# First loads divided over two DMA queues with the input in front, and the first transposes taken token tile by token tile

## Chip, core and metric

One core of one Trainium2 chip runs the whole kernel. The metric is the device time of one execution in microseconds, the median of several runs. The engines are TensorE (PE, with its weight loads shown apart as PEld), VectorE (DVE), ScalarE (ACT), GpSimd (POOL) and SyncE (SP), which here only issues DMAs.

## What is computed

The input `x` is 8 batches of 100 tokens of 512 features, the context 8 x 722 x 512. A decoder layer (self-attention, cross-attention, feed-forward, each with a residual sum and a layer norm) and then a mixture of experts are added to `x`:

```python
x = x + _L0_xattn_ref(_layernorm(x), ctx_1024, ...)
x = x + _L0_ffn_ref(_layernorm(x), Wg, w1, w2)
```

The part that the change touches is the very first: `_layernorm(x)`, and beside it the product of two weight matrices, value projection by output projection (`in_proj_w[2D:]` and `out_proj_w`), which the kernel makes once and uses in place of both.

## The kernel before

All large matrix products run in TensorE's fp32r form in three passes: each fp32 operand is split into a high part (ScalarE copies it, rounding to fp32r) and a low part (VectorE or GpSimd subtracts the high part from the original), and PE multiplies high by high, high by low and low by high. The 800 tokens stand in two halves of 400 (4 batches of 100 tokens). The instructions of each engine are written out in one fixed order, and semaphores tie the engines together; there is no planner. All loads are issued by SyncE on its one queue, in the order of the code.

The head of the program, until PE comes to the first product with the input (`unit(U_Q, 0)`, line 1105), goes as follows.

- **SP** loads quarter 0 and 1 of the two combined weights (`VR` and `OR`, four 256 KB chunks each, `load_vo(0)`, `load_vo(1)`), then the first half of `x` (`load_x_tail(0)`, 32 KB, and `load_x(0)`, `load_x(1)`, 384 KB each, 96 partitions), then `load_vo(2)`, `load_vo(3)`, then the first weights of the query unit (`WR`), the second half of `x`, the constants, and the key weights (`WRK`, 1 MB, line 527).
- **ACT** makes `VH` and `OH` of the four chunks in turn (`split_vo(k)`, lines 1406 and 1408), then half of the first normalisation (token tiles 2 and 3, line 1320), `WH` of the query weights, `XH` of the transposed input (line 1329), more `WH`, then the high part of the combined weights (line 1420), then `WH` of the key weights.
- **DVE** follows with the low parts `VL` and `OL` and, written behind `split_v(1)`, the statistics of the first four token tiles (line 1721), then its half of the normalisation (token tiles 0 and 1, line 1743), then `XL` (line 1759), then two chunks of the query weights' `WL` (line 1917).
- **POOL** makes `OL` of chunks 1 and 3 (`split_o`), the power `rstd` between them (line 636, `inverse_deviation`), and two chunks of the query weights' `WL` (line 642).
- **PE** runs 11 warm-up products on the identity (line 1098), then for each of the four chunks 4 products high by high (`combine_high`, line 929), 4 low by high (line 935) and 4 high by low (line 941). Between the high products and the low products of chunk 3 stand the 16 transposes of the first half of `x` (`to_features(0, 0)`, line 884). They run feature chunk by feature chunk, each over the four token tiles, and every feature chunk is announced as it is done (`to_feat`); `norm_features` on ACT and DVE takes them up one by one.

The second half of the tokens is normalised in the same manner during `unit(U_Q, 0)` and the first group of `unit(U_K, 0)`, and `to_features(0, 1)` (line 1107) transposes it. Its `rstd` on POOL stands behind the key weights' `WL` chunks 2 and 3 (line 707), and these behind ACT's split of the key weights.

Of the kernel before, what the change touches and what calls it, by code (L numbers as in the profile page):

```python
# [7 lines left out]
ALU = mybir.AluOpType  # L8
# [4 lines left out]
P = 128  # L13
B, T, D = 8, 100, 512
# [5 lines left out]
HB = B // 2  # L20
KC = D // P
# [6 lines left out]
TA = T // 16 * 16  # L28
# [144 lines left out]
def build(nc, x, ctxt, ctxn, wvo, wts, consts, g3, be3, out):  # L173
    with ExitStack() as ctx:
        def sem(name):
            return ctx.enter_context(nc.semaphore(name))
# [10 lines left out]
        def sb(name, region, offset, shape, dt=F32):  # L187
            return nc.alloc_sbuf_tensor_at(name, shape, dt, offset=at[region] + offset)
# [19 lines left out]
        tok = sb("tok", "R3", 0, [T, B, D])  # L208
# [37 lines left out]
        VR, OR = [sb(name, "R2", o, [P, KC, D]) for name, o in (("VR", 0), ("OR", 8192))]  # L246
        off = [0]

        def small(name, shape, dt=F32):
            size = 4  # L250
            for s in shape[1:]:
                size *= s
            t = sb(name, "C", off[0], shape, dt)
            off[0] += (size + 31) // 32 * 32
            return t

        ident = small("ident", [P, P])
# [14 lines left out]
        rstd = small("rstd", [T, B])  # L272
# [12 lines left out]
        ps = ctx.enter_context(nc.psum_tensor("ps", [P, 8, 512], F32))  # L285


        x_loaded = [sem("x_loaded%d" % i) for i in range(4)]
        x_tail = [sem("x_tail0"), sem("x_tail1")]
        v_loaded = [sem("v_loaded%d" % k) for k in range(KC)]  # L290
        o_loaded = [sem("o_loaded%d" % k) for k in range(KC)]
# [34 lines left out]
        stats_ready = sem("stats_ready")  # L326
        nmr_ready = sem("nmr_ready")
        tok_ready = sem("tok_ready")
        to_tok = sem("to_tok")
        to_feat = sem("to_feat")  # L330
        x_affine = sem("x_affine")
# [167 lines left out]
        def _(sp):  # L499
            def load_x(i):  # L500
                sp.dma_start(tok[0:TA, 2 * i:2 * i + 2, :], x[2 * i:2 * i + 2, 0:TA].rearrange("b t d -> t b d")
                             ).then_inc(x_loaded[i], 16)

            def load_x_tail(h):

                bs = slice(HB * h, HB * (h + 1))
                sp.dma_start(tok[TA:T, bs, :], x[bs, TA:T].rearrange("b t d -> t b d")).then_inc(x_tail[h], 16)

            def load_vo(k):

                sp.dma_start(VR[:, k, :], wvo[0, :, k, :]).then_inc(v_loaded[k], 16)
                sp.dma_start(OR[:, k, :], wvo[1, :, k, :]).then_inc(o_loaded[k], 16)

            load_vo(0)
            load_vo(1)
            load_x_tail(0)
            load_x(0)
            load_x(1)
            load_vo(2)
            load_vo(3)  # L520
            sp.dma_start(WR[:, 0:2, :], wts[0, :, 0:2, :]).then_inc(w0_loaded, 16)
# [103 lines left out]
        def _(pool):  # L625
# [8 lines left out]
            def inverse_deviation(i, h):  # L634
                pool.wait_ge(stats_ready, i + 1)
                pool.tensor_tensor(rstd[:, HB * h:HB * (h + 1)], veps[:, :], nhalf[:, :],  # L636
                                   ALU.pow).then_inc(rstd_ready, 1)
# [12 lines left out]
            def split_o(k):  # L650

                pool.wait_ge(o_high, k + 1)
                pool.tensor_tensor(OL[:, k, :], OR[:, k, :], raw(OH[:, k, :]), ALU.subtract).then_inc(o_low_pool, 1)
# [45 lines left out]

            split_o(1)  # L700
            inverse_deviation(0, 0)
            pool.wait_ge(nmr_ready, 1)
            split_o(3)
            split_weights(U_Q, range(KC // 2))
            for k in range(KC // 2, KC):
# [48 lines left out]
        def _(pe):  # L754
# [120 lines left out]

            def to_features(i, h, tiles):

                pe.wait_ge(tok_ready, 8 * i + HB * (h + 1))
                if i == 0 and h == 1:
                    pe.wait_ge(vo_low, KC)  # L880
                first = 0 if i == 0 and h == 0 else 4
                for k in range(KC):
                    for j in range(HB):
                        mm = pe.transpose(ps[:, first + k, j * T:(j + 1) * T], tiles[:, j, k * P:(k + 1) * P],  # L884
                                          ident[0:T, 0:T])
                    mm.then_inc(to_feat, 1)

            def to_tokens(i, h, n, src, chunks=range(KC)):

                for k in chunks:  # L890
                    pe.wait_ge(dve_evac, dve_count(n, h, k))
                    if (i, h, k) == (4, 1, KC - 1):
                        pe.wait_ge(out_ready, 2 * HB)
                    for j in range(HB):
                        if (i, h, k, j) == (4, 1, KC - 1, HB // 2):
                            pe.wait_ge(dve_evac, dve_count(n, h, k) + 1)

                        if k:
                            pass
                        elif i == 2 and h == 0:  # L900
                            pe.wait_ge(*((c_exp, B) if j < 2 else (c_probT_low, B)))
                        elif i == 4 and h == 1:
                            pe.wait_ge(out_ready, j + 1)
                        elif h == 1:
                            pe.wait_ge(x_ready, 8 * i + j + 1)
                            if i == 3:
                                pe.wait_ge(x_copied, j + 1)
                        else:
                            pe.wait_ge(x_ready, 8 * min(i, 4))
                        mm = pe.transpose(ps[0:T, 4 + j, k * P:(k + 1) * P], src[h][:, k, j * T:(j + 1) * T],  # L910
                                          ident[:, :])
                        if k == KC - 1 or (i, h, k) == (4, 1, KC - 2):
                            mm.then_inc(to_tok, 1)
# [11 lines left out]
            def combine_high(k):  # L925

                pe.wait_ge(o_high, k + 1)
                for e in range(KC):
                    pe.matmul(ps[:, 4 + e, :], VH[:, k, e * P:(e + 1) * P], OH[:, k, :], start=(k == 0), stop=False)

            def combine_low(k):

                pe.wait_ge(v_low, k + 1)
                for e in range(KC):
                    pe.matmul(ps[:, 4 + e, :], VL[:, k, e * P:(e + 1) * P], OH[:, k, :], start=False, stop=False)
                if k % 2 == 0:
                    pe.wait_ge(o_low, k // 2 + 1)
                else:
                    pe.wait_ge(o_low_pool, k // 2 + 1)
                for e in range(KC):  # L940
                    mm = pe.matmul(ps[:, 4 + e, :], VH[:, k, e * P:(e + 1) * P], OL[:, k, :], start=False,
                                   stop=(k == KC - 1))
                    if k == KC - 1:
                        mm.then_inc(vo_made, 1)
# [146 lines left out]
            tiles = [tok[:, 0:HB, :], tok[:, HB:B, :]]  # L1091
# [7 lines left out]
            for k in range(KC - 1):  # L1099
                combine_high(k)  # L1100
                combine_low(k)
            combine_high(KC - 1)
            to_features(0, 0, tiles[0])
            combine_low(KC - 1)
            unit(U_Q, 0)
            unit(U_K, 0, [0])
# [90 lines left out]
        def _(act):  # L1197
# [116 lines left out]
            def normalise(i, h, dst):  # L1314

                act.wait_ge(nmr_ready, 2 * i + h + 1)
                for j in range(HB // 2, HB):
                    b = HB * h + j
                    src = tok[:, b, :] if i in (0, 3) else ps[0:T, 4 + j, :]
                    act.activation(dst[:, j, :], src, ACT.Identity, bias=nmr[:, b:b + 1],  # L1320
                                   scale=rstd[:, b:b + 1]).then_inc(tok_ready, 1)

            def norm_features(i, h):
                for k in range(KC):
# [76 lines left out]
            tiles = [tok[:, 0:HB, :], tok[:, HB:B, :]]  # L1401
            tiles2 = [tok2[:, 0:HB, :], tok2[:, HB:B, :]]

            def split_vo(k):
                act.wait_ge(v_loaded[k], 16)
                act.activation(VH[:, k, :], VR[:, k, :], ACT.Copy).then_inc(v_high, 1)
                act.wait_ge(o_loaded[k], 16)
                act.activation(OH[:, k, :], OR[:, k, :], ACT.Copy).then_inc(o_high, 1)

            for k in range(KC):  # L1410
                split_vo(k)
            normalise(0, 0, tiles[0])
# [132 lines left out]
        def _(dve):  # L1545
# [188 lines left out]
            def normalise(i, h, dst):  # L1734

                dve.wait_ge(rstd_ready, {0: h, 1: 2 + h, 2: 4 + h, 3: 7 + 2 * h}[i] + 1)
                cols = slice(HB * h, HB * (h + 1))
                dve.scalar_tensor_tensor(out=nmr[:, cols], in0=mv[:, cols, 0], scalar=-1.0, in1=rstd[:, cols],
                                         op0=ALU.mult, op1=ALU.mult).then_inc(nmr_ready, 1)
                for j in range(HB // 2):  # L1740
                    b = HB * h + j
                    src = tok[:, b, :] if i in (0, 3) else ps[0:T, 4 + j, :]
                    dve.tensor_scalar(dst[:, j, :], src, mv[:, b, 0:1], rstd[:, b:b + 1], ALU.subtract,
                                      ALU.mult).then_inc(tok_ready, 1)

            def affine_features(i, h, chunks=(1, 3)):

# [147 lines left out]
            tiles = [tok[:, 0:HB, :], tok[:, HB:B, :]]  # L1895
# [219 lines left out]
```

## Time and profile before

| what | value |
|---|---|
| runs before | 516.28, 516.35, 516.75 us; median 516.35 us |
| the profiled execution | 516.95 us, of which its span (first to last instruction) is 515.1 us |
| PE busy in the span | 505.2 us (98%) |
| DVE, ACT, POOL busy | 374.1, 242.4, 141.4 us (73%, 47%, 27%) |
| DMA | 53.76 MB, 104 GB/s over the span |

The span is what the trace shows; 1.85 us of the profiled execution lie around it. PE's busy share says that nearly all of the time is set by PE; the small rest is idle time of PE, and the rows below show the part of it that lies at the head.

### The profile page before, as it was taken

Reading aid. Unit: us, or ns where it says so; the run is one execution under the profiler, and the core shown is the slowest. Engines: PE = TensorE matmul, PEld = TensorE weight load, DVE = VectorE, ACT = ScalarE, POOL = GpSimd, SP = SyncE. Lnnn points to the kernel's source line nnn. Section 1 sums busy time; section 2 is a strip of 40 time slices with the busy share of each in tenths; the row PEclk is TensorE's granted clock in tenths of the full one; section 3 lists DMA queues with packets and bytes.
Section 4 is the critical chain, followed back from the end, with each engine's and each line's share of the span. In section 5 each row is a group of like instructions: output and inputs, shape, how many; then the busy total and the mean of one; then the engine's idle time right before and its main releaser. Section 6 shows DMA issues by size and latency. Waiting matters only on the chain.

```text
span 515.1 us, 7631 instructions
## 1 busy us (share of the span) xinstructions
PE 505.2 (98%) x2958; PEld 484.4 (94%) x2958; DVE 374.1 (73%) x643; ACT 242.4 (47%) x429; POOL 141.4 (27%) x105
## 2 busy tenths in 40 slices
PE   7999999999999999999999999999999999999997
PEld 6899999889988888989999999999999899999996
DVE  3853769796798986786499877368586878786645
ACT  3853652465598976164554333205437532442210
POOL 2430540014023135154504000805337404030000
PEclk9999999999999999999999999999999999999999
DMA  8951122031689871214522242001301021202004
GB/s 222 337 211 59 59 83 81 1 115 59 223 290 329 298 231 38 81 48 114 92 83 81 83 163 67 16 2 53 111 1 48 36 83 62 102 0 83 1 1 129
DMA packets 18444, 53.76 MB, mean 104 GB/s; under 512 B 1640, under 2 KB 2440, under 8 KB 15848
## 3 DMA queue, kind: packets, MB, share of 16 engines
q1 hardware_dynamic: 18348, 53.20, 31.1%
q8 instruction: 24, 0.39, 0.3%
q14 instruction: 12, 0.10, 0.1%
q10 hardware_dynamic: 60, 0.07, 0.1%
HBM read 51.63 MB, written 1.64 MB: 103 GB/s over the span
## 4 chain that ended last, share of the span: by engine, by line
PE 89%; DVE 4%; DMA 3%; ACT 2%; issue 1%; SPq 0%; POOL 0%; DVEq 0%; ACTq 0%
PE ps L798 17%; PE ps L800 17%; PE ps L799 17%; PE ps L856 5%; PE ps L855 5%; PE ps L854 5%; PE ps L910 2%; PE ps L884 2%; PE ps L1052 2%; PE ps L1053 2%; PE ps L1054 2%; DMA tok<-x_in 2%; PE ps L1026 2%; PE ps L1028 2%; PE ps L1027 2%; PE ps L998 1%
## 5 line engine op out<-in xcount | busy, mean ns | idle before, releaser
L798 PE MATMUL ps<-AH,WH 128*128 128x400 f32 x284 | 98.9, 348 | 1.3 <-DVE AL L1583 1.1
L800 PE MATMUL ps<-AH,WL 128*128 128x400 f32 x284 | 98.0, 345 | 0.0
L799 PE MATMUL ps<-AL,WH 128*128 128x400 f32 x284 | 97.9, 345 | 0.0
L798 PE MATMUL ps<-XH,WH 128*128 128x400 f32 x192 | 66.8, 348 | 0.1
L800 PE MATMUL ps<-XH,WL 128*128 128x400 f32 x192 | 66.3, 345 | 0.0
L799 PE MATMUL ps<-XL,WH 128*128 128x400 f32 x192 | 66.2, 345 | 0.0
L642 POOL TENSOR_TENSOR WL<-WR,WH 128x512 fp32r<-128x512 f32 x30 | 43.3, 1470 | 68.5 <-ACT WH L1217 68.5
L798 PEld LDWEIGHTS ps<-AH,WH 128*128 128x128 f32 x284 | 53.3, 188 | 2.8 <-DVE AL L1583 2.6
L799 PEld LDWEIGHTS ps<-AL,WH 128*128 128x128 f32 x284 | 53.4, 188 | 0.0
L800 PEld LDWEIGHTS ps<-AH,WL 128*128 128x128 f32 x284 | 53.4, 188 | 0.0
L1217 ACT ACTIVATE WH<-WR 128x512 fp32r<-128x512 f32 x60 | 34.1, 624 | 24.3 <-DMA WR<-wts_in 24.3
L1296 ACT ACTIVATE AH<-AT 128x400 fp32r<-128x400 f32 x40 | 21.2, 538 | 49.3 <-DVE AT L1643 32.4
L1605 DVE TENSOR_TENSOR acc<-ps,acc 128x400 f32<-128x400 f32 x47 | 26.7, 570 | 18.7 <-PE ps L800 18.5
L1562 DVE TENSOR_TENSOR ctL<-ctR,ctH 128x1444 fp32r<-128x1444 f32 x16 | 27.9, 1750 | 13.3 <-ACT ctH L1225 13.3
L798 PEld LDWEIGHTS ps<-XH,WH 128*128 128x128 f32 x192 | 36.1, 188 | 0.7 <-issue 0.3
L799 PEld LDWEIGHTS ps<-XL,WH 128*128 128x128 f32 x192 | 36.1, 188 | 0.0
L800 PEld LDWEIGHTS ps<-XH,WL 128*128 128x128 f32 x192 | 36.1, 188 | 0.0
L647 POOL TENSOR_TENSOR cnL<-cnR,cnH 128x1024 fp32r<-128x1024 f32 x7 | 17.0, 2435 | 53.8 <-ACT cnH L1231 53.8
L636 POOL TENSOR_TENSOR rstd<-veps,nhalf 100x4 f32<-100x4 f32 x10 | 14.0, 1395 | 59.3 <-DVE veps L1731 59.0
L1247 ACT ACTIVATE AT<-ps,cst 128x400 f32<-128x400 f32 x16 | 9.5, 595 | 43.7 <-PE ps L800 43.6
L1648 DVE SCALAR_TENSOR_TENSOR AL<-AT,AH 128x400 fp32r<-128x400 f32 x40 | 27.8, 715 | 1.6
L1231 ACT ACTIVATE cnH<-cnR 128x1024 fp32r<-128x1024 f32 x24 | 24.7, 1058 | 1.1 <-DMA cnR<-ctxn_in 1.1
(244 smaller groups left out, 1189.3 us busy)
## 6 DMA issues: line engine op xcount, KB each, us to landing
WR<-wts_in SPq DMA_DIRECT2D x19, 1024.0 KB, 4.8
ctR<-ctxt_in SPq DMA_DIRECT2D x16, 722.0 KB, 5.9
cnR<-ctxn_in SPq DMA_DIRECT2D x16, 512.0 KB, 5.1
cnR<-ctxn_in SPq DMA_DIRECT2D x8, 256.0 KB
tok<-x_in SPq DMA_DIRECT2D x4, 384.0 KB, 10.1
tok<-x_in SPq DMA_DIRECT2D x1, 1536.0 KB
cnR<-ctxn_in SPq DMA_DIRECT2D x8, 160.0 KB
VR<-wvo_in SPq DMA_DIRECT2D x4, 256.0 KB, 6.9
```

Of the source, the lines that this page charges most:

```text
L642: pool.tensor_tensor(WL[SLOT[n]][:, k, :], WR[:, k, :], raw(WH[SLOT[n]][:, k, :]), ALU.subtract).then_inc(w_low_pool, 1)
L798: pe.matmul(dst, wh, half(mh, h, k), start=(k == 0), stop=False)
L799: pe.matmul(dst, wh, half(ml, h, k), start=False, stop=False)
L800: mm = pe.matmul(dst, wl, half(mh, h, k), start=False, stop=(k == KC - 1))
L854: pe.matmul(dst, ah[:, k, cols], bh[:, k, :], start=(k == 0), stop=False)
L855: pe.matmul(dst, ah[:, k, cols], bl[:, k, :], start=False, stop=False)
L856: mm = pe.matmul(dst, al[:, k, cols], bh[:, k, :], start=False, stop=(k == 1))
L1217: act.activation(WH[SLOT[n]][:, k, :], raw_weights[:, k, :], ACT.Copy).then_inc(w_high, 1)
L1231: act.activation(cnH[:, 2 * i:2 * i + 2, :], raw_cn(b, i), ACT.Copy).then_inc(cn_high, 1)
L1562: dve.tensor_tensor(ctL[b % 2][:, 2 * i:2 * i + 2, 0:M], raw_ct(b, i), raw(ctH[b % 2][:, 2 * i:2 * i + 2, 0:M]), ALU.subtract).then_inc(ct ...
L1605: dve.tensor_tensor(half(acc, h, e), src, half(acc, h, e), ALU.add).then_inc(dve_evac, 1)
L1648: dve.scalar_tensor_tensor(out=half(AL, h, e), in0=half(AT, h, e), scalar=0.0, in1=raw(half(AH, h, e)), op0=ALU.max, op1=ALU.subtract).the ...
```

## The change

The first half of `x` is loaded in front of everything else: its first 384 KB and the 32 KB tail by SP, its second 384 KB by ACT's queue, before ACT's first activation. Chunks 0 and 1 of `OR` follow on ACT's queue; the other loads keep their order on SP's. PE's first 16 transposes go token tile by token tile, each tile behind a wait for its own normalisation (new semaphores `first_dve` and `first_act` count tiles 0, 1 and tiles 2, 3), and all four feature chunks are announced during the last tile. POOL's `split_o(3)` waits until DVE has normalised both its tiles, where it waited for the small product `nmr` ahead of them. The orders of ACT's, DVE's and PE's instructions are otherwise the same. The wait in `to_features` drops by four because the first half no longer counts in `tok_ready`.

```diff
+        first_dve, first_act = sem("first_dve"), sem("first_act")
...
-            load_vo(0)
-            load_vo(1)
+            load_x(0)
             load_x_tail(0)
-            load_x(0)
-            load_x(1)
+            load_v(0)
+            load_v(1)
             load_vo(2)
             load_vo(3)
...
             split_o(1)
             inverse_deviation(0, 0)
-            pool.wait_ge(nmr_ready, 1)
+            pool.wait_ge(first_dve, HB // 2)
             split_o(3)
...
             def to_features(i, h, tiles):
-                pe.wait_ge(tok_ready, 8 * i + HB * (h + 1))
+                pe.wait_ge(tok_ready, 8 * i + HB * h)
...
+            def first_features(tiles):
+
+                for j in range(HB):
+                    if j < HB // 2:
+                        pe.wait_ge(first_dve, j + 1)
+                    else:
+                        pe.wait_ge(first_act, j - HB // 2 + 1)
+                    for k in range(KC):
+                        mm = pe.transpose(ps[:, k, j * T:(j + 1) * T], tiles[:, j, k * P:(k + 1) * P],
+                                          ident[0:T, 0:T])
+                        if j == HB - 1:
+                            mm.then_inc(to_feat, 1)
...
             combine_high(KC - 1)
-            to_features(0, 0, tiles[0])
+            first_features(tiles[0])
             combine_low(KC - 1)
...
+            act.dma_start(tok[0:TA, 2:4, :], x[2:4, 0:TA].rearrange("b t d -> t b d")).then_inc(x_loaded[1], 16)
+            for k in range(2):
+                act.dma_start(OR[:, k, :], wvo[1, :, k, :]).then_inc(o_loaded[k], 16)
             for k in range(KC):
                 split_vo(k)
             normalise(0, 0, tiles[0])
```

## Rows read from the trace of the kernel before

**Rows 1.** The page: busy time of each engine.
```profile
PE 505.2 (98%) x2958; PEld 484.4 (94%) x2958; DVE 374.1 (73%) x643; ACT 242.4 (47%) x429; POOL 141.4 (27%) x105
```

**Rows 2.** Timeline of PE, 0 to 21.5 us: start, us, what, idle before.
```profile
1.73 4.27 PE L1098 MATMUL ps<-ident 128*128 128x128 f32 x22 [1.73 <-POOL ones L632]
5.75 1.17 PE L929 MATMUL ps<-OH,VH 128*128 128x512 f32 x4
...
9.20 1.20 PE L929 MATMUL ps<-OH,VH 128*128 128x512 f32 x4 [0.46 <-ACT OH L1408]
10.23 1.07 PE L935 MATMUL ps<-OH,VL 128*128 128x512 f32 x4
11.14 1.07 PE L941 MATMUL ps<-OL,VH 128*128 128x512 f32 x4
...
17.98 1.59 PE L884 MATMUL ps<-ident,tok 100*128 100x100 f32 x16 [0.38 <-DVE tok L1743]
...
19.36 1.17 PE L935 MATMUL ps<-OH,VL 128*128 128x512 f32 x4
...
21.29 0.34 PE L798 MATMUL ps<-XH,WH 128*128 128x400 f32 x1
```

**Rows 3.** The chain that ended last, in order of time: start, us, what.
```profile
3.37 8.47 DMA tok<-x_in
...
32.41 1.38 PE ps L884 x16
```

**Rows 4.** Timeline of ACT, 0 to 32 us.
```profile
4.80 0.63 ACT L1408 ACTIVATE OH<-OR 128x512 fp32r<-128x512 f32 x1 [0.21 <-DMA OR<-wvo_in]
7.15 0.63 ACT L1406 ACTIVATE VH<-VR 128x512 fp32r<-128x512 f32 x1 [1.72 <-DMA VR<-wvo_in]
8.51 0.63 ACT L1408 ACTIVATE OH<-OR 128x512 fp32r<-128x512 f32 x1 [0.73 <-DMA OR<-wvo_in]
12.32 0.63 ACT L1406 ACTIVATE VH<-VR 128x512 fp32r<-128x512 f32 x1 [3.18 <-DMA VR<-wvo_in]
...
18.58 1.69 ACT L1329 ACTIVATE XH<-ps 128x400 fp32r<-128x400 f32 x4
...
23.88 2.20 ACT L1217 ACTIVATE WH<-WRK 128x512 fp32r<-128x512 f32 x4 [0.51 <-DMA WRK<-wts_in]
...
30.53 1.52 ACT L1320 ACTIVATE tok<-tok,nmr,rstd 100x512 f32<-100x512 f32 x2 [1.87 <-DVE nmr L1738]
```

**Rows 5.** Timeline of DVE, 0 to 22 us.
```profile
10.48 2.67 DVE L1721 BATCH_NORM_STATS2 bnst<-tok 100x6 f32<-100x512 f32 x4 [1.97 <-DMA tok<-x_in]
...
15.95 1.98 DVE L1743 TENSOR_SCALAR tok<-tok,mv,rstd 100x512 f32<-100x512 f32 x2
...
21.05 1.28 DVE L1917 TENSOR_TENSOR WL<-WR,WH 128x512 fp32r<-128x512 f32 x2
```

**Rows 6.** Windows: width, busy and (count) of PE, PEld, DVE, ACT, POOL, clock, DMA share, GB/s.
```profile
1.73:5.75 4.02, 4.02 (x22) 4.02 (x23) 0.98 (x2) 1.55 (x3) 0.41 (x1) 1.00 0.81 206
5.75:8.75 3.00, 2.98 (x15) 2.16 (x13) 1.09 (x2) 0.87 (x2) 0.00 (x0) 1.00 0.98 263
...
12.21:13.68 1.47, 0.00 (x0) 0.00 (x0) 1.40 (x8) 1.26 (x3) 0.00 (x0) 1.00 1.07 405
```

**Rows 7.** Windows, later stretch, while line 601 reloads all of x alone.
```profile
245.00:247.00 2.00, 2.00 (x13) 2.00 (x12) 0.00 (x0) 0.47 (x1) 1.92 (x2) 1.00 1.06 236
```

**Rows 8.** The warm-up's line: weight loads, ns min/median/max.
```profile
L1098 PEld LDWEIGHTS ps<-ident x22: 192/333/338, 1.7 to 5.6; 128*128 128x128 f32 x22
```

**Rows 9.** Tile tok: DVE's half of the normalisation, ns min/median/max.
```profile
L1743 DVE TENSOR_SCALAR tok<-tok,mv,rstd x4: 540/542/1519, 16.0 to 30.9; 100x512 f32<-100x512 f32 x4
```

**Rows 10.** Timeline of POOL, 0 to 21 us.
```profile
16.12 1.53 POOL L653 TENSOR_TENSOR OL<-OR,OH 128x512 fp32r<-128x512 f32 x1 [0.28 <-DVE nmr L1738]
18.19 2.74 POOL L642 TENSOR_TENSOR WL<-WR,WH 128x512 fp32r<-128x512 f32 x2 [0.55 <-ACT WH L1217]
```

**Rows 11.** Timeline of SP: its first DMA issue.
```profile
0.74 0.38 SPq L511 DMA_DIRECT2D VR<-wvo_in  x1
```

More of the change, by code:

```diff
@@ L507, in load_x_tail, with load_v @@
                 sp.dma_start(tok[TA:T, bs, :], x[bs, TA:T].rearrange("b t d -> t b d")).then_inc(x_tail[h], 16)
+            def load_v(k):
+                sp.dma_start(VR[:, k, :], wvo[0, :, k, :]).then_inc(v_loaded[k], 16)
             def load_vo(k):
-                sp.dma_start(VR[:, k, :], wvo[0, :, k, :]).then_inc(v_loaded[k], 16)
+                load_v(k)
                 sp.dma_start(OR[:, k, :], wvo[1, :, k, :]).then_inc(o_loaded[k], 16)
-            load_vo(0)
-            load_vo(1)
+            load_x(0)
             load_x_tail(0)
-            load_x(0)
-            load_x(1)
+            load_v(0)
+            load_v(1)
             load_vo(2)
@@ L876, in to_features @@
             def to_features(i, h, tiles):
-                pe.wait_ge(tok_ready, 8 * i + HB * (h + 1))
+                pe.wait_ge(tok_ready, 8 * i + HB * h)
                 if i == 0 and h == 1:
                     pe.wait_ge(vo_low, KC)
-                first = 0 if i == 0 and h == 0 else 4
                 for k in range(KC):
                     for j in range(HB):
-                        mm = pe.transpose(ps[:, first + k, j * T:(j + 1) * T], tiles[:, j, k * P:(k + 1) * P],
+                        mm = pe.transpose(ps[:, 4 + k, j * T:(j + 1) * T], tiles[:, j, k * P:(k + 1) * P],
                                           ident[0:T, 0:T])
                     mm.then_inc(to_feat, 1)
+            def first_features(tiles):
[9 more added lines that the diff above has]
+                            mm.then_inc(to_feat, 1)
             def to_tokens(i, h, n, src, chunks=range(KC)):
@@ L1320, in normalise @@
                     act.activation(dst[:, j, :], src, ACT.Identity, bias=nmr[:, b:b + 1],
-                                   scale=rstd[:, b:b + 1]).then_inc(tok_ready, 1)
+                                   scale=rstd[:, b:b + 1]).then_inc(first_act if (i, h) == (0, 0) else tok_ready, 1)
             def norm_features(i, h):
@@ L1743, in normalise @@
                     dve.tensor_scalar(dst[:, j, :], src, mv[:, b, 0:1], rstd[:, b:b + 1], ALU.subtract,
-                                      ALU.mult).then_inc(tok_ready, 1)
+                                      ALU.mult).then_inc(first_dve if (i, h) == (0, 0) else tok_ready, 1)
             def affine_features(i, h, chunks=(1, 3)):
```

## The prediction

> **What bounds the kernel now.** I read the page first: PE is busy for 505.2 of 515.1 us [rows 1], so a change is worth what it adds to or takes from PE's idle time, or what it does to the one stretch where PE waits for loads. That stretch is the head. PE's timeline there [rows 2] shows the warm-ups to about 5.75 us, the weight product from 5.75, waits of 0.46 us for `OH` of chunk 1 and of 1.47 us for chunk 2 [rows 2, 6], and 0.38 us ahead of the transposes, which begin at T = 17.98. These 2.3 us are all that better loading could give. `unit(U_Q, 0)` begins at 21.29 and the next hard dependency is the second block of transposes at 32.41 [rows 3].
>
> ACT's timeline [rows 4] then tells when loads land, as ACT takes each chunk up at once: `OR` 0 by 4.80 us, `VR` 1 by 7.15, `OR` 1 by 8.51, `VR` 2 by 12.32. The chain [rows 3] ends the second quarter of x at 3.37 + 8.47 = 11.84. In all of this the DMA engines are 0.8 to 1.07 busy [rows 6]: the head is bound by bytes in a queue, and their order decides.
>
> **The loads.** The weight product's first step needs `OH` 0, so `VR` 0 and `OR` 0. Before, 512 KB had to land for it. After, 384 + 384 + 32 KB of x are ahead of, and 512 KB with, these two: 1312 KB or 1.34 MB. Three readings of when that has landed:
> - Lowest. `OR` 0 landed at 4.8 after 0.52 MB; at the 405 GB/s of an x-free stretch [rows 6] that is 1.3 us of data, so the queue's dead time ends at 3.5. The two quarters of x took 11.84 - 8.51 = 3.34 us [rows 3, 4]; 0.79 MB in that time is 235 GB/s, and the reload of x alone, much later, runs at the same 236 [rows 7]. So x is a slow load in itself, and ends at 6.8. `VR` 2 stood 0.5 us behind the end of x before, and one more chunk costs 0.65: `OR` 0 at 8.0.
> - Bytes moved. 4.02 us x 206 = 0.83 MB by 5.75, then 263 GB/s [rows 6]: 1.34 MB moved at 7.7. Landing lags behind that: 1.05 MB (through `OR` 1) would be moved at 6.6 and landed at 8.5, 1.9 us later, since some engines run ahead. This gives 9.6.
> - Highest. Landing against bytes as it was: 1024 KB at 8.51, 1824 KB at 11.84, so 1312 KB at 9.7, with the tail at most 9.9.
>
> I take 8.8, between the first and the other two, as the start of x no longer mixes with chunks 1. Then ACT makes `VH` and `OH`: 0.67 us behind the landing if `VR` 0 is a little ahead, 1.3 us if both land together, which two queues with the same bytes ahead make likely. So the product starts at S = 9.9 where it was 5.75; bounds 8.7 and 11.2.
>
> **From there.** With no wait a chunk costs 2.85 us (9.20 to 12.05: a first group of 1.03, then 0.91 each [rows 2]), the next ones 3 x 0.91 = 2.73, the high group of chunk 3 0.91: 2.85 + 2.73 + 2.73 + 0.91 = 9.2. Chunk 1 is needed at S + 2.85 = 12.8, when ACT has long split it (four activations of 0.67 from 8.8 end at 11.5), and the rest of the queue runs at 405 GB/s; so the three waits, 2.3 us, do go. T becomes 9.9 + 9.2 = 19.1: +1.1 us. Bounds by S: 17.9 (-0.1) and 20.4 (+2.4).
>
> **x in front buys little by itself.** DVE's order is unchanged: the statistics stand behind `split_v(1)`, and that waits for ACT's third activation, `VH` 1, at about 10.6. `VL` 1 ends at about 11.3, so statistics start at about 11.3 where they started at 10.48 [rows 5]. From there to the normalisation it took 5.47 us (15.95 - 10.48 [rows 5]): 16.8, and the four tiles are ready at about 18.3. PE comes at 19.1 and doesn't wait. 0.8 us of cover; without it, with S at 8.7, all moves together and the cover is the same, since both hang on the same loads.
>
> **POOL's wait.** DVE's two tiles took 1.98 us [rows 5], one of them 1519 ns where the other three of this line took 540 [rows 9], while POOL's `OL` 3 ran from 16.12 to 17.65 [rows 10]. With POOL held back DVE needs 1.1 us: 0.9 us less on the way to the transposes, hidden here as PE is late. `OL` 3 ends 1.5 us behind DVE, at about 19.4; PE needs it at T + 1.4 + 0.9 = 21.4. Behind it on POOL stand the two `WL` of the query weights, 2.74 us [rows 10]: to 22.2, the first to about 20.8; PE wants them at 22.8 and 23.3. Covered. The Trainium skill, in "SBUF — State Buffer", section "Who interferes with whom", says that VectorE in its two-port modes and GpSimd lock each other out for a whole instruction; the 1519 ns agree, and the sum is the same without the rule.
>
> **ACT's issues.** Three DMA issues of about 0.4 us [rows 11] stand ahead of ACT's first activation, which has nothing to read before 4 us. Free.
>
> **Tile by tile.** The 16 transposes cost the same 1.38 us (17.98 to 19.36 [rows 2]). No tile is late, so the finer waits win nothing. But feature chunk 0 is announced after 13 of 16 instead of after 4 of 16: 9 x 0.086 = 0.78 us later relative to T. `XH` then starts at T + 1.38 (was 18.58 = T + 0.60 [rows 4]) and everything behind it on ACT and DVE moves too. `WL` 2 on DVE (21.05 [rows 5], T + 3.07) now starts at T + 3.85 and ends at T + 4.53; PE's third product of that chunk stands at T + 3.31 + 8 x 0.18 = T + 4.77. 0.24 us of cover, and 0.18 for `WL` 3. Further on, ACT reached the key weights at 23.37 and waited 0.51 us for them [rows 4]; now it is there at T + 5.39 + 0.78 = T + 6.17. From that start to the last normalised tile of the second half it took 30.53 + 1.52 - 23.88 = 8.17 us, so T + 14.34; PE wants it at T + 14.43 (32.41 [rows 3]). I put 0.1 us there, bounds 0 and 0.6 (if the 0.78 is paid in full again).
>
> **Sum.** +1.1 + 0.1 = +1.2 us on the profiled execution's 516.95 (span 515.1 and 1.85 around it), 518.15; the median stands 0.6 lower, so 516.35 + 1.2 = 517.6 us. Behind 33 us nothing differs and PE runs full, so the shift stays to the end. Own range of this case: S from 9.2 (T 18.4, +0.4) to 11.2 (+2.4), with the stall of 0 to 0.6: 516.8 to 519.3.
>
> **Rivals.**
> - *The clock falls.* PE is idle from 5.9 to about 9.9, 4 us; before, its longest pause was 1.47 us and its speed held. At the start, weight loads took 333 ns and from about 5 us on 192 [rows 8], the levels 1.2 and 2.4 GHz, though the clock column reads 1.00; it took some 3.2 us of work (1.73 to 5) to rise. The same again on the weight product, at half pace: +1.5 us, in all +2.7, 519.1. For: the pause is far longer than any seen. Against: no row shows a fall. The Trainium skill, "TensorE: Matmul & The Clock Gate", Part 1, has PE go back to 1.2 GHz after idling; no row of this trace shows it.
> - *The new order costs nothing.* The loads come near the low bound, S 8.7 to 9.2, and the waits removed pay for the late start: +0 to +0.5, 516.6.
> - *Faster.* Two queues move x faster than one. If x went at 405 GB/s as the chunks do, it would save 1.4 us of 3.34, and S is below 7.7; T is then 1.1 us or more earlier. It decides from S = 7.8. But the key weights at 23.86 bind next: without them also earlier, only 32.41 - 32.05 = 0.36 us is kept. With them, -1.2: 515.1. For: the two queues overlap the dead time of x. Against: the DMA engines show full shares with one queue already [rows 6, 7]. The Trainium skill, "DMA: Bandwidth & Descriptors", "Issuing engines are not separate DMA queues", says that several issuers save only issue time; nothing here shows two at once.
>
> **Chances.** What a measurement can tell is about 0.2%, 1.0 us. Forecast case 0.46 (of it 0.13 below +1.0), clock 0.17, nothing 0.25, faster 0.12. So faster 0.12, same 0.38, slower 0.50. Range 516.0 to 519.4, which leaves out most of the faster case and the worst of the clock.
>
> **What the changed profile would show.** First `OH` ending near 9.9 and PE idle from 5.9 to there, no idle time between chunks, transposes at about 19.1 with no wait on tiles, DVE's two tiles at 0.54 us each, `XH` 1.4 us behind the first transpose, the second transposes at about 33.6. The prediction is wrong if `OR` 0 lands before 7.5 or after 10, if weight loads of chunk 0 take 333 ns, or if statistics start later than 12 us, so that PE waits for tiles after all.

## The result and the profile after

The changed kernel takes 519.25 us (median of 6 runs, 518.67 to 519.66), the kernel before 516.65 us (median of 6 runs, 516.28 to 517.12). The ratio is 1.0048 with a 95% interval of 1.0037 to 1.0058: slower by 2.6 us. The forecast was 517.6 us, with a range of 516.0 to 519.4 and a chance of 0.50 for slower. The sign and the range hold; the shift is more than twice the 1.2 us of the forecast.

The page of the kernel after, busy time of each engine, answers to [rows 1]:

```profile
PE 506.8 (98%) x2958; PEld 486.2 (94%) x2958; DVE 372.9 (72%) x643; ACT 242.0 (47%) x429; POOL 141.3 (27%) x105
```

PE is busy for 1.6 us longer than before, with the same 2958 products, so some of them took longer. The timeline of PE (start, us, what, idle before) answers to [rows 2]:

```profile
1.73 4.88 PE L1114 MATMUL ps<-ident 128*128 128x128 f32 x22 [1.73 <-POOL ones L636]
10.16 2.08 PE L945 MATMUL ps<-OH,VH 128*128 128x512 f32 x4 [3.55 <-ACT OH L1424]
12.03 1.59 PE L951 MATMUL ps<-OH,VL 128*128 128x512 f32 x4
13.46 1.09 PE L957 MATMUL ps<-OL,VH 128*128 128x512 f32 x4
14.39 1.07 PE L945 MATMUL ps<-OH,VH 128*128 128x512 f32 x4
...
20.75 1.54 PE L899 MATMUL ps<-ident,tok 100*128 100x100 f32 x16
22.06 1.18 PE L951 MATMUL ps<-OH,VL 128*128 128x512 f32 x4
...
24.00 0.34 PE L802 MATMUL ps<-XH,WH 128*128 128x400 f32 x1
```

The warm-ups alone took 0.61 us longer (4.88 against 4.27 us); with 11 products they took 4.1 to 5.1 us in the profiles of this case, and the first chunk's start hangs on the loads here, not on them. The first chunk starts at 10.16 where it started at 5.75, after a pause of 3.55 us. Its groups of four take 2.08 and 1.59 us instead of 1.17 and 1.07, so that chunk 1 starts 4.23 us behind chunk 0 instead of 2.85. From then on no group waits: the three waits of before are gone. The windows (width, busy and count of PE, PEld, DVE, ACT, POOL, clock, DMA share, GB/s) show why the first chunk is slow:

```profile
5.00:6.00 1.00, 1.00 (x7) 1.00 (x7) 0.00 (x0) 0.00 (x0) 0.00 (x0) 1.00 1.09 172
...
7.00:8.00 1.00, 0.00 (x0) 0.00 (x0) 0.00 (x0) 0.00 (x0) 0.00 (x0) 1.00 1.06 373
...
9.00:10.00 1.00, 0.00 (x0) 0.00 (x0) 0.38 (x1) 1.00 (x2) 0.00 (x0) 0.86 1.05 389
10.00:11.00 1.00, 0.84 (x2) 0.75 (x3) 1.00 (x3) 1.00 (x3) 0.00 (x0) 0.50 1.08 397
...
12.00:13.00 1.00, 1.00 (x4) 0.78 (x3) 1.00 (x3) 1.00 (x3) 0.66 (x1) 0.50 1.02 410
13.00:14.00 1.00, 1.00 (x6) 0.83 (x5) 0.96 (x3) 0.23 (x1) 0.00 (x0) 0.94 1.02 379
```

The granted clock is 0.50, that is 1.2 GHz, from about 9.7 us (0.86 is the mean of that microsecond) to about 13.1 us, and full again behind that. The reader should also keep the first of these rows: the DMA engines are fully busy from 5 to 6 us and move only 172 GB/s. That row turns out to matter most.

ACT and DVE, answering to [rows 4, 5]:

```profile
8.96 0.63 ACT L1422 ACTIVATE VH<-VR 128x512 fp32r<-128x512 f32 x1 [5.50 <-DMA VR<-wvo_in]
9.49 0.61 ACT L1424 ACTIVATE OH<-OR 128x512 fp32r<-128x512 f32 x1
...
16.82 1.52 ACT L1336 ACTIVATE tok<-tok,nmr,rstd 100x512 f32<-100x512 f32 x2 [3.59 <-DVE nmr L1757]
...
22.06 1.69 ACT L1345 ACTIVATE XH<-ps 128x400 fp32r<-128x400 f32 x4 [2.68 <-PE ps L899]
...
26.68 2.25 ACT L1233 ACTIVATE WH<-WRK 128x512 fp32r<-128x512 f32 x4
```

```profile
11.43 2.46 DVE L1740 BATCH_NORM_STATS2 bnst<-tok 100x6 f32<-100x512 f32 x4
...
16.70 1.00 DVE L1762 TENSOR_SCALAR tok<-tok,mv,rstd 100x512 f32<-100x512 f32 x2
```

`VR` 0 lands at 8.94 us, `OR` 0 had landed at 7.3 and waits for ACT to split `VR` 0 first, x is there long before anybody asks, and the statistics start 0.95 us later than before. The chain, answering to [rows 3], runs through the load of `VR`, and has the second transposes at 35.52 where they were at 32.41:

```profile
1.59 7.35 DMA VR<-wvo_in
...
35.52 1.38 PE ps L887 x16
```

Between the first and the second transposes lie 35.52 - 20.75 = 14.77 us, before 32.41 - 17.98 = 14.43: 0.34 us more. (The chain puts the start of the second block 0.16 us later than the timeline does, in both kernels; by the timeline alone it is 35.36 - 20.75 = 14.61 and 32.25 - 17.98 = 14.27, with the same difference.) Behind the second ones the rest takes 517.7 - 35.52 = 482.2 us, before 515.1 - 32.41 = 482.7. The whole change lies in the first 36 us.

### The profile page after: what moved, and what is told of

Read it like the earlier page. It is cut to its first block, busy times and chain, and to the rows that moved or that the text cites. A ratio compares the mean times of both kernels' runs of the same rounds, so it can differ in the third digit from the quotient of the medians.

```text
span 517.7 us, 7631 instructions
## 1 busy us (share of the span) xinstructions
PE 506.8 (98%) x2958; PEld 486.2 (94%) x2958; DVE 372.9 (72%) x643; ACT 242.0 (47%) x429; POOL 141.3 (27%) x105
## 4 chain that ended last, share of the span: by engine, by line
PE 94%; DVE 2%; DMA 1%; ACT 1%; issue 0%; SPq 0%; DVEq 0%; ACTq 0%
PE ps L802 17%; PE ps L804 17%; PE ps L803 17%; PE ps L860 5%; PE ps L859 5%; PE ps L858 5%; PE ps L926 2%; PE ps L1068 2%; PE ps L1070 2%; PE ps L1069 2%; PE ps L1042 2%; PE ps L1044 2%; PE ps L1043 2%; PE ps L887 2%; DMA VR<-wvo_in 1%; PE ps L1014 1%
## 6 DMA issues: line engine op xcount, KB each, us to landing
tok<-x_in SPq DMA_DIRECT2D x3, 384.0 KB, 10.6
```

## The experiments

Times of each are given with the ratio to the kernel before on the same chip, since that is what the interval is for. "T" is the start of the first transposes, 17.98 before and 20.75 after.

### More warm-up products: is it the clock?

```diff
-WARM_UP = 11
+WARM_UP = 26
```

> The changed kernel with 26 warm-up products in place of 11, so that PE works until about 10 us, when the first chunk is split. Theory (the pause lets TensorE's clock fall to 1.2 GHz and the first chunk pays for it): chunk 0 of the weight product takes 2.85 us instead of 4.23, the granted clock stays 1.00 from 9 to 13 us, and the time is 1.2 to 1.4 us below the changed kernel's: 517.9. Rival (chunk 0 is slow because it waits for the low parts, or the clock costs nothing in the end because the input is late anyway): within 0.3 us of 519.25.

Measured: 518.17 us, ratio 1.0033 (1.0022 to 1.0045). The timeline of PE:

```profile
1.74 8.66 PE L1114 MATMUL ps<-ident 128*128 128x128 f32 x52 [1.74 <-POOL ones L636]
10.16 1.18 PE L945 MATMUL ps<-OH,VH 128*128 128x512 f32 x4
11.17 1.08 PE L951 MATMUL ps<-OH,VL 128*128 128x512 f32 x4
...
19.35 1.54 PE L899 MATMUL ps<-ident,tok 100*128 100x100 f32 x16
```

The first chunk starts at the same 10.16 and now costs 2.83 us; T is 19.35, exactly 1.40 us earlier. With PE kept busy the clock stays up, so the fall costs 1.4 us of the head. That the start is the same is chance. ACT's timeline shows that `OH` 0 was ready at 9.34 in this execution:

```profile
8.73 0.61 ACT L1424 ACTIVATE OH<-OR 128x512 fp32r<-128x512 f32 x1
```

The long warm-up itself held the chunk back by 0.8 us. The total moved by 1.1 us by the medians and 0.8 us by the ratios, whose intervals overlap. That this is less than 1.4 us fits such a warm-up, which takes something away wherever the loads land earlier than they did in the changed kernel's profile; it is argued, not shown. The profile is that of the slowest of the 12 runs (520.75 us). It had two waits of 0.7 and 0.5 us in the cross-attention that the changed kernel's did not show, and I can't say whether they belong to the edit.

### No warm-up products

The changed kernel with `WARM_UP = 0`.

> The changed kernel without warm-up products. Theory (the clock has fallen by the time PE gets its first chunk, so the warm-ups are wasted): the first chunk runs at 1.2 GHz as in the changed kernel, 519.0 to 520.0. Rival (the warm-ups still shorten the slow stretch): 520.5 or more.

Measured: 520.4 us (4 runs, 519.33 to 521.8), ratio 1.0076 (1.0057 to 1.0095). In the one profile the first chunk started at 9.44, its groups took 2.05 and 1.91 us as at 1.2 GHz (the column of the granted clock reads 1.00 there, as it does at the start of every trace of this case, so the durations tell it), and T was 20.59. The head was no worse than the changed kernel's while the runs were worse by 1.1 us. The range lies between the two theories; this one decides nothing.

### The loads alone, the tiles alone

The changed kernel with the old order of the transposes and the old wait on GpSimd:

```diff
-            pool.wait_ge(first_dve, HB // 2)
+            pool.wait_ge(nmr_ready, 1)
...
-                for j in range(HB):
-                    if j < HB // 2:
-                        pe.wait_ge(first_dve, j + 1)
-                    else:
-                        pe.wait_ge(first_act, j - HB // 2 + 1)
-                    for k in range(KC):
+                pe.wait_ge(first_dve, HB // 2)
+                pe.wait_ge(first_act, HB // 2)
+                for k in range(KC):
+                    for j in range(HB):
```

> The changed kernel's loads alone: transposes again feature chunk by feature chunk behind all four tiles, GpSimd's wait as before. Theory (the loads are the whole loss; PE comes to the transposes late, so their order is hidden): within 0.3 us of the changed kernel, 518.9 to 519.6, with XH starting 0.6 us behind the first transpose instead of 1.3. Rival (the tile order is a part of the loss): 0.5 us or more below the changed kernel.

Measured: 519.24 us, ratio 1.0049 (1.0037 to 1.0062), the same as the changed kernel. In its profile PE started at 9.53 and the clock stayed at 0.50 until about 15.4 us, so that T was 21.46, 11.93 us behind the start instead of the changed kernel's 10.59. DVE's two tiles took 1.98 us again, and nobody noticed, as PE came to the transposes 3 us after them. `XH` started 0.55 us behind the first transpose, against 1.31 with the tiles, and the second transposes came 14.38 us behind the first, against 14.77.

The other half, the loads as before with tiles and GpSimd's new wait:

```diff
-            load_x(0)
-            load_x_tail(0)
-            load_v(0)
-            load_v(1)
+            load_vo(0)
+            load_vo(1)
+            load_x_tail(0)
+            load_x(0)
+            load_x(1)
             load_vo(2)
```

(and ACT's three DMA issues removed)

> The kernel before with its loads as they were, and only the transposes tile by tile and GpSimd's wait for both of VectorE's tiles. Theory (this part is worth the wait of 0.38 us ahead of the transposes and no more, and it was hidden in the changed kernel): transposes begin at 17.5 instead of 17.98, VectorE's two tiles take 0.54 us each, and the time is 516.2 to 516.4, 0.3 to 0.4 below before. Rival (announcing the feature chunks 0.78 us later holds up what comes next and gives the gain back, or more): 516.65 to 517.4.

Measured: 516.57 us, ratio 1.0000 (0.9992 to 1.0009). In its profile DVE's two tiles took 1.00 us and PE did not wait for them:

```profile
13.14 1.19 PE L946 MATMUL ps<-OH,VH 128*128 128x512 f32 x4 [0.44 <-ACT OH L1425]
...
16.91 1.54 PE L900 MATMUL ps<-ident,tok 100*128 100x100 f32 x16
```

The loads of that one execution also landed half a microsecond earlier (`VR` 2 at 11.78 instead of 12.32), so T can't be held against 17.98 alone. The 0.3 us that I expected is smaller than the interval's half width of 0.4 us. So the tile part neither costs nor wins anything that can be measured, and the loads are the whole loss.

### x in front, on one queue

SP alone issues x 0, tail, x 1, `VR` 0, `OR` 0 and on.

> The changed kernel with all loads on SP's queue, the first half of x in front: x 0, tail, x 1, VR 0, OR 0, VR 1, OR 1 and on. Theory (the bytes ahead of the first chunk set its landing, whichever queue they stand in): first OH ends between 9.7 and 10.7, the clock falls as in the changed kernel, 519.0 to 519.8. Rival (the division over two queues lets other loads in between and delays VR 0): first OH by 9.2, 1 us less, and 517.5 to 518.3.

Measured: 519.97 us (6 runs, 518.83 to 521.51), ratio 1.0069 (1.0052 to 1.0086). The timeline of PE and the windows:

```profile
9.36 1.20 PE L946 MATMUL ps<-OH,VH 128*128 128x512 f32 x4 [2.56 <-ACT OH L1425]
10.39 1.67 PE L952 MATMUL ps<-OH,VL 128*128 128x512 f32 x4
```

```profile
10.00:11.00 1.00, 1.00 (x5) 0.79 (x4) 0.61 (x2) 0.96 (x2) 0.00 (x0) 0.83 1.06 406
11.00:12.00 1.00, 1.00 (x4) 0.81 (x3) 1.00 (x3) 0.91 (x3) 0.86 (x1) 0.50 1.07 424
```

The division over two queues is not what costs: one queue is no faster. The first `OH` ended at 9.3, between what the two sides had expected, and the time lies above both. Still the clock fell, at about 10.7 us (0.83 is the mean of that microsecond), 1.3 us after PE had taken up its work again and after a pause of only 2.56 us. The second quarter of x landed at 1.61 + 5.4 = 7.0 here and at 0.74 + 5.3 = 6.0 on ACT's queue in the changed kernel, so in these two profiles two queues brought x in 1 us earlier; the first chunk gained nothing by it.

### Two queues, the weights in front

```diff
-            load_x(0)
-            load_x_tail(0)
             load_v(0)
             load_v(1)
+            load_x_tail(0)
+            load_x(0)
             load_vo(2)
...
-            act.dma_start(tok[0:TA, 2:4, :], x[2:4, 0:TA].rearrange("b t d -> t b d")).then_inc(x_loaded[1], 16)
             for k in range(2):
                 act.dma_start(OR[:, k, :], wvo[1, :, k, :]).then_inc(o_loaded[k], 16)
+            act.dma_start(tok[0:TA, 2:4, :], x[2:4, 0:TA].rearrange("b t d -> t b d")).then_inc(x_loaded[1], 16)
```

> The changed kernel with the weights in front on both queues: SP issues VR 0, VR 1, tail, x 0, and ACT issues OR 0, OR 1, x 1. Theory (the order of the bytes costs the time, not the second queue): first OH by 5.7 us, PE starts the weight product right behind its warm-ups, the clock stays up, chunk 1 doesn't wait, chunk 2 waits 1 to 2 us for VR 2 and OR 2, and the time is 516.0 to 516.5, at or below before. Rival (two queues taking turns are themselves what delays the loads): first OH at 7 us or later, 517.5 or more.

Measured: 516.63 us, ratio 1.0007 (0.9994 to 1.0019). PE starts at 6.34 right behind its warm-ups, chunk 1 doesn't wait, chunk 2 waits 0.81 us for `OH` and 0.72 us for `VL`, T is 17.68. The first `OH` ended at 6.28, later than the 5.7 of the theory and earlier than the 7 of the rival. The loss is gone. The version with the tiles alone has the same order of loads on one queue and measured 1.0000 (0.9992 to 1.0009): with the weights in front the second queue makes no difference that these runs can measure. With x in front the tail's place, told below, stands in the way of that comparison; one queue with x in front and the tail behind the weights was not run.

### One queue, chunk 2 ahead of x as well

SP's order is `VR`/`OR` 0, 1, 2, tail, x 0, x 1, and on DVE `split_v(2)` and `split_o(2)` stand ahead of the statistics.

> One queue, the other direction: chunks 0, 1 and 2 of the weights ahead of x, VectorE's low parts of chunk 2 ahead of the statistics, tiles as in the changed kernel. Theory (PE starts at 5.7 to 6.5 and must not wait for chunk 2; x is needed only for tiles at 17): chunks 0 to 2 without a wait, the statistics end near 14.3, the transposes start at 17.0 to 17.5, 515.7 to 516.3. Rival (x late now sets the transposes): they start at 18.0 or later, 516.6 to 517.5.

Measured: 516.76 us, ratio 1.0003 (0.9994 to 1.0012).

```profile
15.22 1.21 PE L946 MATMUL ps<-OH,VH 128*128 128x512 f32 x4 [1.15 <-ACT OH L1425]
...
17.14 1.71 PE L900 MATMUL ps<-ident,tok 100*128 100x100 f32 x16 [0.70 <-DVE tok L1760]
```

Chunks 0 to 2 run without a wait, as meant. The wait moves to chunk 3 (1.15 us, behind x in the queue) and to the tiles (0.70 us). The transposes start at 17.14, within the theory's range, and the time does not follow: 516.76 where 515.7 to 516.3 were expected. The profile is that of the slowest of the 11 runs, and shows PE waiting another 0.45 us for `WL` of GpSimd in `unit(U_Q, 0)`. Each of these orders makes something else late.

### The tail of x, moved back

In the changed kernel `VR` 0 landed at 8.94 but `OR` 0 at 1.19 + 6.1 = 7.3, although each queue had one 384 KB load ahead. The only thing besides was the 32 KB tail on SP's queue.

```diff
             load_x(0)
-            load_x_tail(0)
             load_v(0)
             load_v(1)
+            load_x_tail(0)
             load_vo(2)
```

> The changed kernel with the 32 KB tail of x behind VR 0 and VR 1 on SP's queue. VR 0 landed 1.6 us behind OR 0 in the changed kernel, though each queue had the same large load ahead. Theory (the tail's few engines hold VR 0 up): VR 0 lands at 7.5 to 8.2, PE starts at 8.7 to 9.4, 518.0 to 518.6. Rival (VR 0 lands late for the bytes alone): VR 0 within 0.3 us of 8.94, and 519.0 to 519.5.

Measured: 516.35 us, ratio 0.9997 (0.9987 to 1.0007): the whole loss is gone, 2.6 us for moving 32 KB behind 512 KB. PE, then ACT, then the windows:

```profile
8.10 1.21 PE L945 MATMUL ps<-OH,VH 128*128 128x512 f32 x4 [1.31 <-ACT OH L1424]
...
17.35 1.54 PE L899 MATMUL ps<-ident,tok 100*128 100x100 f32 x16
```

```profile
6.90 0.63 ACT L1422 ACTIVATE VH<-VR 128x512 fp32r<-128x512 f32 x1 [3.45 <-DMA VR<-wvo_in]
...
9.30 0.63 ACT L1422 ACTIVATE VH<-VR 128x512 fp32r<-128x512 f32 x1 [1.25 <-DMA VR<-wvo_in]
```

```profile
5.00:6.00 1.00, 1.00 (x7) 1.00 (x7) 0.00 (x0) 0.00 (x0) 0.00 (x0) 1.00 1.02 305
...
8.00:9.00 1.00, 0.90 (x4) 0.75 (x5) 0.86 (x2) 0.05 (x1) 0.00 (x0) 1.00 1.12 168
```

`VR` 0 lands at 6.9 instead of 8.94. The slow spell of 170 GB/s has moved with the tail, from 5 to 6 us to 8 to 9 us. PE's pause is 1.31 us and the clock doesn't fall. The expected 518.0 was too high: it left out that a shorter pause also gives the clock's 1.4 us back, and `VR` 0 landed 0.6 us before the earliest time expected. The size is not that of one pair of profiles alone: with the tail ahead of it `VR` 0 landed at 8.1 to 8.9 in four profiles, with the tail behind `VR` 1 at 6.4 to 6.9 in three, so the tail costs it 1.2 to 2.6 us.

The same tail on the other queue, between x 1 and `OR` 0:

```diff
             act.dma_start(tok[0:TA, 2:4, :], x[2:4, 0:TA].rearrange("b t d -> t b d")).then_inc(x_loaded[1], 16)
+            act.dma_start(tok[TA:T, 0:HB, :], x[0:HB, TA:T].rearrange("b t d -> t b d")).then_inc(x_tail[0], 16)
```

> The changed kernel with the tail of x on ACT's queue, between x 1 and OR 0, instead of on SP's ahead of VR 0. Theory (the tail delays what stands behind it on its own queue): VR 0 lands near 7, as with the tail late, but OR 0 near 8.5 to 9, PE starts at 9 to 10, the clock falls, 518.7 to 519.5. Rival (only SP's queue suffers, or the tail was not it): PE starts by 8.5, 516.2 to 517.5.

Measured: 520.11 us, ratio 1.0071 (1.0058 to 1.0084). ACT's timeline:

```profile
7.22 0.63 ACT L1421 ACTIVATE VH<-VR 128x512 fp32r<-128x512 f32 x1 [3.25 <-DMA VR<-wvo_in]
9.52 0.63 ACT L1423 ACTIVATE OH<-OR 128x512 fp32r<-128x512 f32 x1 [1.66 <-DMA OR<-wvo_in]
```

Now `VR` 0 is early and `OR` 0 late: whatever stands behind the tail on its own queue pays. PE starts at 10.20 after a pause of 3.48 us, the clock is 0.50 from 10 to 13 us, T is 20.89. So the tail is what makes the first chunk late, on whichever queue it stands.

### The tail at the very front

The order of the kernel before on one queue, with the tail as the first load of all, and the tiles.

> One queue, the order of the kernel before, but the 32 KB tail of x as the very first load; tiles as in the changed kernel. Theory (the tail costs about 1 us of the queue wherever it stands, and at the very start the warm-up products cover it): the slow spell is over by 4 us, PE starts at 6 to 6.7, the wait for chunk 2 shrinks below 0.8, transposes at 16.2 to 16.8, 515.4 to 516.0. Rival (the tail costs the same there, it only moves what is late): transposes at 17.3 or later, 516.3 to 517.

Measured: 517.08 us, ratio 1.0008 (0.9998 to 1.0019), at T = 18.24, with a wait of 1.63 us for chunk 2. The rival holds: with the tail in front the chunks land 0.6 to 1.3 us later than in the kernel before (`VR` 0 at 5.28 instead of 3.96, `OR` 1 at 9.14 instead of 8.51), and nothing is won for it.

### No pause and no tail

The changed kernel with the tail behind `VR` 1 and `WARM_UP = 17`.

> The changed kernel with the tail behind VR 0 and VR 1, and 17 warm-up products, so that PE has no pause at all before its first chunk. Theory (with a pause of only 1.3 us the clock had not fallen, so there is nothing left to win): within 0.3 us of 516.35. Rival (in some executions the pause was longer and the clock fell): 0.4 us or more below it.

Measured: 516.19 us, ratio 0.9993 (0.9984 to 1.0001). PE has no idle time at all from 1.73 to 90 us, and T is 17.16. It is 0.25 us below the kernel before, and the interval still touches 1.

### The same with the transposes by feature chunk

The last version, with the 16 transposes feature chunk by feature chunk behind all four tiles, as in the edit of "The loads alone" but with GpSimd's new wait kept.

> The version with the tail behind VR 1 and 17 warm-up products, but the 16 transposes again feature chunk by feature chunk, behind all four tiles (GpSimd's new wait is kept). In every version with tiles the second transposes stood 14.77 us behind the first, in the two with feature chunks 14.38 to 14.43. Theory (PE waits for WL 2 ahead of the first product of its chunk, and the late announcement of the feature chunks makes WL 2 late by 0.35 us): 14.4 us here, and a time 0.3 to 0.4 below the version with tiles, 515.8, below the kernel before by more than its interval. Rival (the 0.35 us has another cause, or is lost again behind): 14.7 us or more, or the same time as with tiles, 516.2.

Measured: 516.55 us beside 516.82 for the kernel before in these rounds, ratio 0.9989 (0.9976 to 1.0001), against 0.9993 with the tiles. The timeline of PE and the chain:

```profile
16.36 1.07 PE L942 MATMUL ps<-OH,VH 128*128 128x512 f32 x4
17.57 1.56 PE L897 MATMUL ps<-ident,tok 100*128 100x100 f32 x16
```

```profile
31.98 1.38 PE ps L887 x16
```

The distance is 31.98 - 17.57 = 14.41 us, as the theory has it, and no gain over the version with the tiles shows, as the rival has it. (Of the versions with tiles the one with chunk 2 ahead of x does not have the 14.77 us that I wrote there: its distance is 32.64 - 17.14 = 15.50, with the wait for GpSimd in it.) PE had finished the high products at about 17.3 and waited some 0.3 us for the last tile. So both are true, as far as one profile of each tells: tile by tile takes up the tiles 0.3 us earlier and gives 0.35 us back in `unit(U_Q, 0)`. Neither this version nor the one with tiles beats the kernel before beyond its interval.

## Why the prediction was right or wrong

- *Loads.* Forecast: `OR` 0 and `VR` 0 landed at 8.8, PE's start at 9.9 (8.7 to 11.2). Measured: 8.94 for `VR` 0 and 10.16. The number was right by luck, and the step behind it failed. I counted the tail by its 32 KB, 0.08 us at 405 GB/s and 0.2 us at most, where it costs `VR` 0 1.2 to 2.6 us. Moved away, it gives 6.9 and 7.3 for the two landings, below my lowest reading of 8.0, and a start at 8.10. Nor did `VR` 0 and `OR` 0 land together, which I had called likely: `OR` 0 was there at 7.3, before the 7.5 that I had named as a sign of being wrong, and the 1.2 us from the landing to the start are ACT's two activations behind the late `VR` 0. The three readings all took the kernel before as it was, where bytes and rates don't separate the tail. That kernel has a slow spell of its own at 4 to 6 us (166 and 186 GB/s), but the version with chunk 2 ahead of x has it too (182 GB/s from 4 to 5 us) with its tail 512 KB further back, so it is not the tail's; what the tail costs the kernel before stays open.
- *The waits that go.* Right: 9.2 us from PE's start to T was the forecast, and with the clock up it is 19.35 - 10.16 = 9.19; in the version with the tail late 17.35 - 8.10 = 9.25. But 2.3 us was not all that better loading could give, as I wrote: the way was 12.23 us before and 9.19 without waits, 3.04 us less, since each wait costs more than its idle time. A group of four costs 0.91 us in a row and 1.03 behind a wait, and the group ahead of a wait has 0.16 us more to run out (1.07 against 0.91).
- *The clock.* This is the second step that failed, and the one that the sum shows. It was put as a rival at 0.17 with +1.5 us; it happened, and cost 1.40. Half the shift is this. The place and the mechanism were those of the rival, the chance was too low. The other sign of being wrong came with it: the weight loads of the chunk's first group took 338 ns. The head then adds up: +4.41 for the later start, -3.04 for the shorter way from there to T (12.23 before, 9.19 without waits), +1.40 for the clock: +2.77, which is 20.75 - 17.98. The forecast had +1.1 for the first two; they were +1.37.
- *Which pauses matter.* The pauses of 1.31, 1.48 and 1.63 us left the clock alone; those of 2.56, 3.46, 3.48 and 3.55 us did not. The trace of before showed only the first kind, and from it I gave a fall a chance of 0.17. The Trainium skill, "TensorE: Matmul & The Clock Gate", Part 1, has the clock return to 1.2 GHz after idling, and the runs agree.
- *DVE and POOL.* Right. DVE's two tiles take 1.00 us instead of 1.98 once GpSimd waits for them, and it was hidden. The statistics started at 11.43 (11.3).
- *Tile by tile.* Half right. `XH` starts 1.31 us behind the first transpose (1.38), the finer waits win nothing in the changed kernel, and nobody waits at the second transposes, where I had put 0.1 us. But 0.34 us are lost on the way there, and the cover of 0.24 us for `WL` 2 was reckoned to the wrong instruction: I took the third product of the chunk, which reads `WL`, while `unit` waits for `WL` ahead of all three (`wait_w_low` in the loop over `k`). `WL` 2 is ready at 25.2 and the chunk's first product follows:

```profile
24.92 0.34 PE L804 MATMUL ps<-XH,WL 128*128 128x400 f32 x1
25.36 0.42 PE L802 MATMUL ps<-XH,WH 128*128 128x400 f32 x1
```

  Two products in a row start 0.18 us apart when nothing waits; here it is 0.44. The forecast's step of 0.1 us was therefore 0.34, at another place.
- *Faster by the second queue.* It did not come. x was in 1 us earlier than on one queue, but even with the tail moved away the start was 8.10, 7.96 and 8.02, never the 7.8 from which this rival was to decide, and the first transposes came 0.4 to 0.8 us earlier than before without a gain that can be measured. The Trainium skill, "DMA: Bandwidth & Descriptors", "Issuing engines are not separate DMA queues", has several issuers save only issue time; the two versions with the weights in front, on one queue and on two, measured 1.0000 and 1.0007 of the kernel before and agree. The landing of x, 6.0 against 7.0, is not told by that rule.
- *The sum.* +2.77 at the first transposes, +0.34 to the second, -0.5 behind them (482.2 us against 482.7, about what two executions differ by): +2.6 in the span and in the medians.

## What to carry to other kernels

Ahead of the first work of the bounding engine, count what stands in front of its operands in the queue, and don't count a small load by its bytes alone: 32 KB over 4 partitions held up the load behind it by 1.2 to 2.6 us. Whether its shape does this or any small load would is not shown; no run had 32 KB in another shape. A late start is paid twice when the pause lets TensorE's clock fall, so extend the warm-up to the first operand's landing and no further, or better bring that operand forward. Look up where a wait stands in the code before reckoning its cover: a wait ahead of three instructions binds the first. Here, with the DMA engines full, every other order of the loads moved the wait, and none beat the kernel before.

## What the runs showed of the hardware that I had not expected

- A load of 32 KB over 4 partitions (16 rows of 2 KB) makes a spell of about 1 us in which the DMA engines are fully busy (1.07 to 1.18) and move 162 to 188 GB/s, in seven of the eight profiles with the changed kernel's loads (242 in the eighth); with the tail moved back, the same microsecond has 305 to 322. `VR` 0 behind it on its own queue lands 1.2 to 2.6 us late and `OR` 0 2.2 us (9.5 instead of 7.3, its issue 0.6 us later), the chunk on the other queue by far less (`OR` 0 at 7.2 to 7.4 whether the tail stood ahead of `VR` 0 or behind `VR` 1; `VR` 0 at 7.2 with the tail on ACT's queue, against 6.4 to 6.9). That the few engines it runs on are the cause is a guess; no run here shows shares by engine.
- The clock fell in the one-queue version at about 10.7 us, when PE had been back at work since 9.36, after a pause of 2.56 us. In the versions where the clock fell it was back at full speed between 13.1 and 15.4 us, and the way from PE's start to T was 10.6 to 11.9 us instead of 9.2: 1.4 to 2.7 us for a fall.
- The landing of the same first load in kernels with the same loads varied between executions: `VR` 0 at 8.94, 8.3, 8.2 and 8.1 us in the changed kernel and its three variants with equal queues.
